# Cross attention of a decoder kernel: queries by three fp32r products instead of one fp32 product, with the tokens' rests on GpSimd

## The reference

```python
Q = (x @ Wq + bq)              # 4096 tokens x 256, 16 heads of 16
K, V = split(ctx @ Wkv + bkv)  # 4 x 77 tokens
attn = softmax(Q K^T * 16**-0.5 (+ mask))
x = layernorm(x + (attn V) @ Wo + bo)
```

## Time and profile before

| | |
|---|---|
| runs | 2994.00, 3000.15, 3001.02 us |
| median | 3000.15 us |
| the profiled execution's own time | 2996.25 us |
| its span in the profile | 2994.5 us |
| mean granted clock of PE | 0.942 of 2.4 GHz |

### The profile page before, as it was taken

How to read it: one execution, slowest core, us unless ns; L and a number is a source line. 1 busy time by engine, 2 the same in 40 slices (tenths; PEclk the granted TensorE clock), 3 DMA queues, 4 the chain that set the end, 5 groups by cost and what they waited for, 6 DMA issues and landing times. The chain is left out here.

```text
span 2994.5 us, 43256 instructions
## 1 busy us (share of the span) xinstructions
PE 2639.8 (88%) x11953; PEld 1603.3 (54%) x11953; DVE 1699.4 (57%) x3404; ACT 1175.7 (39%) x1644; POOL 1574.1 (53%) x1309
## 2 busy tenths in 40 slices
PE   7999999999999999999999968882796588788696
PEld 5666666666666666666666533432474244343254
DVE  5665665656666665665666634663234555468743
ACT  3443444444444444444444324541222334344234
POOL 3666766767766677676777731224333313222343
PEclk8999999999999999999999979996898599899798
DMA  6554455554556445455554320003894100000233
GB/s 174 115 130 111 105 121 114 120 116 110 113 114 135 108 111 120 106 121 114 122 115 106 68 82 9 2 2 116 334 339 144 45 0 1 30 2 9 49 124 91
DMA packets 407008, 303.17 MB, mean 101 GB/s; under 512 B 293559, under 2 KB 338911, under 8 KB 401791
## 3 DMA queue, kind: packets, MB, share of 16 engines
q1 hardware_dynamic: 390734, 231.17, 32.9%
q0 software_dynamic: 12224, 64.71, 6.1%
q10 hardware_dynamic: 3952, 6.08, 0.6%
HBM read 187.04 MB, written 94.39 MB: 94 GB/s over the span
## 5 line engine op out<-in xcount | busy, mean ns | idle before, releaser
L655 POOL TENSOR_TENSOR a_total<-a_total,a_pr 128x1024 f32<-128x1024 f32 x384 | 914.0, 2380 | 55.9 <-ACT a_pr L639 35.1
L639 ACT ACTIVATE a_pr<-a_psS 128x1024 f32<-128x1024 f32 x512 | 525.3, 1027 | 670.3 <-PE a_psS L627 666.5
L584 DVE TENSOR_REDUCE a_nmax<-a_psX 128x1 f32<-128x512 f32 x1024 | 695.4, 688 | 157.4 <-PE a_psX L579 155.8
L667 PE MATMUL a_psO<-a_pr,a_vd 128*64 128x512 f32 x2048 | 481.8, 602 | 0.0
L579 PE MATMUL a_psX<-a_kA,a_qA 128*128 128x512 f32 x1024 | 413.1, 405 | 25.6 <-issue 12.6
L655 POOL TENSOR_TENSOR a_total<-a_pr 128x1024 f32<-128x1024 f32 x64 | 153.5, 2399 | 482.0 <-ACT a_pr L639 482.0
L627 PE MATMUL a_psS<-a_qA,a_kA 128*128 128x512 f32 x1024 | 338.9, 412 | 2.7 <-DVE a_nT L600 1.4
L627 PE MATMUL a_psS<-a_qB,a_kB 128*128 128x512 f32 x1024 | 321.2, 395 | 0.0
L667 PEld LDWEIGHTS a_psO<-a_pr,a_vd 128*64 128x64 f32 x2048 | 129.9, 136 | 236.5 <-issue 179.3
L579 PEld LDWEIGHTS a_psX<-a_kA,a_qA 128*128 128x128 f32 x1024 | 194.0, 190 | 105.8 <-issue 35.9
L627 PEld LDWEIGHTS a_psS<-a_qA,a_kA 128*128 128x128 f32 x1024 | 180.9, 189 | 123.1 <-issue 90.1
(11 more groups left out here) (390 smaller groups left out, 4344.7 us busy)
## 6 DMA issues: line engine op xcount, KB each, us to landing
a_qA<-a_qhi SPq DMA_DIRECT2D x124, 256.0 KB
a_vd<-a_vg SPq DMA_DIRECT2D x128, 128.0 KB
a_kA<-a_khi SPq DMA_DIRECT2D x62, 256.0 KB
a_kA<-a_klo SPq DMA_DIRECT2D x62, 256.0 KB
a_kB<-a_khi SPq DMA_DIRECT2D x62, 256.0 KB
a_qB<-a_qlo SPq DMA_DIRECT2D x62, 256.0 KB
a_qhi<-a_ph SPq DMA_DIRECT2D x120, 128.0 KB, 3.1
a_qlo<-a_pl SPq DMA_DIRECT2D x120, 128.0 KB, 2.9
```

The lines of the kernel that those rows point to most:

```text
L584: w.eng.tensor_reduce(nmax[:, half, u:u + 1], psX[:, half, :], AX.X, ALU.max, negate=True)\
L639: w.eng.activation(pr[:, n, :], psS[:, half, :, :].rearrange("p a b -> p (a b)"), ACT.Exp, scale=SCALE)\
L655: w.eng.tensor_tensor(total[:, buf, :], first, pr[:, n, :], ALU.add).then_inc(sems["ad"], 1)
L667: last = w.eng.matmul(psO[q * HD:(q + 1) * HD, :], vd[:, b, kc, :], pr[:, n, q * 512:(q + 1) * 512], start=kc == 0, stop=kc == KC - 1)
```

## The change

In both cross attentions:

- `queries` no longer multiplies fp32 data. The weights and the turned tokens are each split into a part rounded to fp32r and the rest, and three products are summed in the bank: rounded weights by rounded tokens, rest of the weights by rounded tokens, rounded weights by the tokens' rest. That makes six matmuls of one pass where there were two of two passes.
- The weights are split once, in a new step `split_weights` after `turn_context`: ACT copies `wq` (128 x 1024) to `wqh`, POOL subtracts into `wql`.
- In `turn_x` ACT now copies the bank twice (to `xT` and, rounded, to `xh`), and POOL subtracts the two into `xl` for each half. `queries` waits on PE for `xl` of the second half (a semaphore of POOL), where it waited for ACT's copies.
- The four small POOL operations of `outputs` become a step of their own, `root`. For the first half it is called after `turn(1)` and thus stands on POOL behind the rests of both halves; for the second half it stays behind `put(1)`.
- To make room, `cx` lies in `xT`, and `wq` and `wk` in `oT`.

```diff
@@ -906,7 +906,7 @@
 
     with ExitStack() as ctx:
         m = Room(nc, ctx, tag)
-        wq, wk = (m.sb(n, [P, 2, NQ * P]) for n in ("wq", "wk"))
+        wqh, wql = (m.sb(n, [P, 2, NQ * P], F32R) for n in ("wqh", "wql"))
         wv, wo = (m.sb(n, [P, 2, D]) for n in ("wv", "wo"))
         bq, bk = (m.sb(n, [P, NQ]) for n in ("bq", "bk"))
         bqs, bks = (m.sb(n, [P, NQ]) for n in ("bqs", "bks"))
@@ -914,7 +914,6 @@
         bo = m.sb("bo", [P, D])
         ident = m.sb("ident", [P, P])
         sel0, sel17 = (m.sb(n, [P, 1]) for n in ("sel0", "sel17"))
-        cx = m.sb("cx", [TK, B, D])
         cxT = m.sb("cxT", [P, 2, B * TK])
         mraw = m.sb("mraw", [P, B * TK // 4], mybir.dt.int32)
         mbias = m.sb("mbias", [P, B, TK])
@@ -923,6 +922,10 @@
         kblk = m.sb("kblk", [P, NQ, B, NQ, TK], F32R)
         vP = m.sb("vP", [TK, B, H, R])
         xT = m.sb("xT", [P, 2, BT])
+        xh, xl = (m.sb(n, [P, 2, BT], F32R) for n in ("xh", "xl"))
+        cx = xT[0:TK, :, :].rearrange("p a b -> p (a b)").rearrange("p (b c) -> p b c", c=D)
         qF = m.sb("qF", [P, 3, NQ, BT])
         qR = m.sb("qR", [P, 2, NQ, BT], F32R)
         nmx = m.sb("nmx", [P, 4, H])
@@ -932,6 +935,7 @@
         inv = m.sb("inv", [P, BT // R])
         oC = m.sb("oC", [P, BT])
         oT = m.sb("oT", [P, 2, 2, BT])
+        wq, wk = oT[:, 0, :, :], oT[:, 1, :, :]
         xb = m.sb("xb", [P, 2, 2, D])
         res = m.sb("res", [P, 2, 2, D])
         bst = m.sb("bst", [P, 2, 2, 6])
@@ -944,7 +948,7 @@
         psS = m.ps("psS", [P, NQ, 512])
         psO = m.ps("psO", [P, 512])
         psM = m.ps("psM", [P, RB, 512])
-        names = ("cst", "cstv", "x", "cx", "wk", "wq", "wv", "wo", "mi", "m0", "m1", "m2", "k", "kf", "kb", "qr", "qm", "s",
+        names = ("cst", "cstv", "x", "cx", "wk", "wq", "wv", "wo", "wh", "wl", "xh", "xl", "mi", "m0", "m1", "m2", "k", "kf", "kb", "qr", "qm", "s",
                  "ex", "pv", "tk", "dv", "ot", "xb", "var", "pl", "rstd", "y")
         sems = {n: m.sem(n) for n in names}
         block = ctx.enter_context(nc.Block())
@@ -982,6 +986,15 @@
                 w.eng.tensor_copy(mb[:, :], psM[0:TK, k, 0:B * P:P]).then_inc(sems[f"m{k}"], 1)
             w.inc(f"m{k}")
             came["mask"] = (f"m{k}", w.at(f"m{k}"))
+        def split_weights(w):
+            if w.on("scalar"):
+                w.wait("wq", 16)
+                w.eng.activation(wqh[:, :, :], wq, ACT.Copy).then_inc(sems["wh"], 1)
+            if w.on("gpsimd"):
+                w.wait("wh", 1)
+                w.eng.tensor_tensor(wql[:, :, :], wq, wqh[:, :, :].bitcast(F32), ALU.subtract).then_inc(sems["wl"], 1)
 
         def keys(w):
             if w.on("tensor"):
@@ -1048,22 +1061,30 @@
                                                X[:, 4 * n + 2 * half + tt, cc * P:(cc + 1) * P], ident[:, :])
                 last.then_inc(sems["mi"], 1)
             w.inc("mi")
+            cols = slice(half * 256, (half + 1) * 256)
             if w.on("scalar"):
                 w.wait("mi", w.at("mi"))
-                w.eng.activation(xT[:, :, half * 256:(half + 1) * 256], psM[:, k, :].rearrange("p (a b) -> p a b", a=2), ACT.Copy)\
-                    .then_inc(sems[f"m{k}"], 1)
+                w.wait("xl", w.at("xl", 1))
+                w.eng.activation(xT[:, :, cols], psM[:, k, :].rearrange("p (a b) -> p a b", a=2), ACT.Copy).then_inc(sems["xh"], 1)
+                w.eng.activation(xh[:, :, cols], psM[:, k, :].rearrange("p (a b) -> p a b", a=2), ACT.Copy).then_inc(sems[f"m{k}"], 1)
+            w.inc("xh")
             w.inc(f"m{k}")
-            came["x", half] = (f"m{k}", w.at(f"m{k}"))
+            if w.on("gpsimd"):
+                w.wait("xh", w.at("xh"))
+                w.wait(f"m{k}", w.at(f"m{k}"))
+                w.eng.tensor_tensor(xl[:, :, cols], xT[:, :, cols], xh[:, :, cols].bitcast(F32), ALU.subtract).then_inc(sems["xl"], 1)
+            w.inc("xl")
 
         def queries(w, n, c):
             k = bank(w)
             if w.on("tensor"):
-                w.wait("wq", 16)
-                for half in range(2):
-                    w.wait(*came["x", half])
+                w.wait("wl", 1)
+                w.wait("xl", w.at("xl"))
                 w.wait(f"m{k}", w.at(f"m{k}"))
-                for cc in range(2):
-                    last = w.eng.matmul(psM[:, k, :], wq[:, cc, c * P:(c + 1) * P], xT[:, cc, :], start=cc == 0, stop=cc == 1)
+                for i, (wp, xp) in enumerate(((wqh, xh), (wql, xh), (wqh, xl))):
+                    for cc in range(2):
+                        last = w.eng.matmul(psM[:, k, :], wp[:, cc, c * P:(c + 1) * P], xp[:, cc, :],
+                                            start=i == 0 and cc == 0, stop=i == 2 and cc == 1)
                 last.then_inc(sems["mi"], 1)
             w.inc("mi")
             if w.on("scalar"):
@@ -1208,10 +1229,12 @@
                 w.inc("dv")
             w.inc(f"m{k}")
             w.inc("var")
+        def root(w, n, half):
             if w.on("gpsimd"):
                 if n or half:
                     w.wait("y", w.at("y"))
-                w.wait("var", w.at("var"))
+                w.wait("var", 2 * n + half + 1)
                 w.link(w.eng.tensor_tensor(rstd[:, half, 0, :], mv[:, half, :, 1], eps[:, :], ALU.add), "pl")
                 w.link(w.eng.tensor_tensor(rstd[:, half, 1, :], rstd[:, half, 0, :], mhalf[:, :], ALU.pow), "pl")
                 w.link(w.eng.tensor_tensor(rstd[:, half, 2, :], mv[:, half, :, 0], rstd[:, half, 1, :], ALU.mult), "pl")
@@ -1295,6 +1318,10 @@
                 if n:
                     outputs(w, n - 1, half)
 
+            def roots(half):
+                if n:
+                    root(w, n - 1, half)
             def norm(half):
                 if n:
                     normed(w, n - 1, half)
@@ -1311,6 +1338,7 @@
             scores(w, n, 1)
             big((0, 3))
             turn(1)
+            roots(0)
             big((1, 0), (1, 1))
             also(0)
             values(w, n, 0)
@@ -1325,6 +1353,7 @@
             values(w, n, 1)
             big((2, 3), (3, 0))
             put(1)
+            roots(1)
             big((3, 1), (3, 2))
             scores(w, n, 3)
             big((3, 3))
@@ -1344,6 +1373,7 @@
         def walk(w):
             for cc in range(2):
                 turn_context(w, cc)
+            split_weights(w)
             keys(w)
             for half in range(2):
                 turn_x(w, 0, half)
@@ -1372,6 +1402,7 @@
                 hall.load(w, 0)
             for half in range(2):
                 outputs(w, NB - 1, half)
+                root(w, NB - 1, half)
             for half in range(2):
                 normed(w, NB - 1, half)
             if hall is not None:
@@ -1380,8 +1411,8 @@
 
         @block.sync
         def _(eng):
-            eng.dma_start(cx[:, :, :], kv.rearrange("b k c -> k b c")).then_inc(sems["cx"], 16)
-            eng.dma_start(wk[:, :, :], w_k.rearrange("(a p) o -> p a o", p=P)).then_inc(sems["wk"], 16)
+            eng.dma_start(cx, kv.rearrange("b k c -> k b c")).then_inc(sems["cx"], 16)
+            eng.dma_start(wk, w_k.rearrange("(a p) o -> p a o", p=P)).then_inc(sems["wk"], 16)
             if y is not None:
                 eng.dma_start(X[:, 0:4, :], y.rearrange("(t p) c -> p t c", p=P)[:, 0:4, :]).then_inc(sems["x"], 16)
             eng.dma_start(wv[:, :, :], w_v.rearrange("(a p) o -> p a o", p=P)).then_inc(sems["wv"], 16)
@@ -1432,7 +1463,7 @@
                 eng.dma_start(t[:, :], src).then_inc(sems["wk"], 16)
             if mask is not None:
                 eng.dma_start(mraw[:, :], mask.partition_broadcast(P)).then_inc(sems["wk"], 16)
-            eng.dma_start(wq[:, :, :], w_q.rearrange("(a p) o -> p a o", p=P)).then_inc(sems["wq"], 16)
+            eng.dma_start(wq, w_q.rearrange("(a p) o -> p a o", p=P)).then_inc(sems["wq"], 16)
             eng.dma_start(wo[:, :, :], w_o.rearrange("(a p) o -> p a o", p=P)).then_inc(sems["wo"], 16)
             eng.dma_start(bo[:, :], b_o.partition_broadcast(P)).then_inc(sems["wo"], 16)
             eng.preload_act_table(ACT.Exp)
```

## The result

The changed kernel takes 3029.12 us (median of 4 runs, 3022.24 to 3033.45) where the kernel before takes 2997.07 us in the same session: a ratio of 1.0109, 95% interval [1.0095, 1.0124], 32 us more. The profiled execution took 3022.24 us, the fastest of its four.

A forecast was written before the change was run, and what follows sets the result against it. PE was taken to bound the stage, busy 24.8 of a block's 27.75 us. The chain's +14 us and the clock's +15 us gave +29 us: 3025 us profiled, 3029 us at the median, range 3003 to 3050 us.

The forecast's parts named there:

- Steps A to D: Blocks 1 to 5 of each attention: shorter queries save 1.36 us, waits for `xl` and `qF` lose 2.7: +1.3 a block.
- rival 3: POOL's subtraction is as quick as its rounding (0.61 us) and the clock holds: +7 us, 3007 us; chance 0.13.
- The start: Ahead of each attention's blocks: queries begin 2.4 us later for copies and subtractions, four calls give back 1.36: +1.0 us.
- Block 0 and block 6: In each attention: block 0, without `normed`, +0.3 us; block 6, inheriting only the shorter last queries, -0.7 us.
- The clock: PE's idling lets its clock fall to 0.50 at half of 14 places: 7 x 2.2 = +15 us.
- steps B and C: In a block: first `queries` wait for `xl`, 1.0 us later; the late root frees `qF`'s bank 1.65 us late.
- Rival 1: PE's clock stays up in both attentions: +14 us, 3014 us; chance 0.25.
- Rival 4: Rests ready before PE asks in each block: 21.8 us saved whole, less 2 for the start, 2980 us; chance 0.10.

The follow-up runs named there:

- root back: Changed kernel with the root called right behind `outputs` again, on POOL ahead of both rests: 3034.96 us, ratio 1.0132 to the kernel before.
- late wait: Changed kernel with PE waiting for `xl` only before the third product of `queries`: 3026.54 us, ratio 1.0109 to the kernel before.
- early turn: Changed kernel with the second half's transposes ahead of the second `scores`: 3008.65 us, ratio 1.0045 to the kernel before.
- the run with PE kept at work: Changed kernel, root left late, with six unread matmuls on PE before the wait for `xl`: 3018.05 us, ratio 1.0081 to the kernel before.
- the best order: Changed kernel with root back, late wait, both halves turned ahead of the second `scores`, scalings behind the queries' copy: 2980.09 us, ratio 0.9969.

## Why the prediction came out right, and where it did not

**Steps A to D.** Right, nearly to the tenth. Predicted: 2.0 us of idling for `xl`, measured 2.05; about 1.6 us for `qF`, measured 1.50; a block at full clock of 29.05, measured 29.11. POOL's subtraction took 1.26 to 1.28 us in the blocks, as the row with two operands said, which ended rival 3. The separate edits confirm the links: root back, the second wait goes; late wait, it moves; early turn, the first goes.

**The start.** The term of +1.0 us a start was mis-sized: it measured +4.0 and +3.4. I had PE's start 2.4 us late; in the first attention it was 2.9 late (1779.26 is 19.66 us behind the identity's first operation, at 1759.60; 1780.80 was 16.76 behind its own at 1764.04), since two subtractions beside DVE took 2.95 us, not 2.56; in the second it was 2.6 late. And the four calls gave nothing back: behind 3.89 us of idling the clock was at half for the first 3 us, as the window below shows, and the 24 passes took from 1779.26 to 1786.65, 7.4 us against 7.11 before. In the kernel without these rests they took 5.84 us at full clock, so 1.5 us of each start belong to the clock. The last 0.8 and 0.6 us I did not foresee: behind these queries PE waits for banks that ACT now copies twice, 0.89 and 0.67 us in the first attention (at 1789.32 and 1792.22) where it had waited 0.40 and 0.18 (at 1790.09 and 1792.50).

```profile
1779.20:1782.40 3.20, 3.14 (x8) 2.53 (x9) 3.01 (x7) 0.41 (x1) 0.00 (x0) 0.55 0.37 126
```

**Block 0 and block 6.** Predicted +0.3 and -0.7; the two block 0 were -1.6 and +0.4, and block 6 with what follows -1.1 and -1.9. Small, and they hide part of the start's error.

**The clock.** The number of falls was about right (7 of 14 places forecast, 9 found: both starts, blocks 2, 3 and 5 of the first attention and 1, 2, 4 and 5 of the second), the price was not. By the table, blocks 1 to 5 grew by 20.5 us in both attentions; ten times 1.36 is 13.6 of it, so the clock took some 7 us of these blocks, and with 3.1 in the starts some 10 us of the profiled execution, not 15. Two things were mis-sized. A short stretch at 0.50 (some 3 us) cost 0.2 to 0.4 us, in the blocks of 29.30 and 29.48; a long one (some 7 us) cost 1.8, in that of 30.94. I had 2.2 for all. The short ones were cheap because a wait took them up: in the block of 29.30 the slower queries came ahead of the wait for `qF`, which fell from 1.50 to 0.36 us (at 1908.84). And I priced block 1 as a new place, though it had the end of such a stretch in it already. The medians are 6 us further apart than the profiled executions (32 and 26 us); the changed kernel's runs spread over 11 us, and which of its blocks fall may differ between them, which no profile here shows.

**The sum.** Measured in the attentions: 13.6 for the ten blocks, 7.4 for the starts (3.1 of it the clock's), 7 for the clock in the blocks, -4.1 for blocks 0, 6 and the ends: 23.9, and 2.1 elsewhere. Forecast: +29, of which 14 by the chain and 15 by the clock. That the total came out near is luck, since errors stood against each other: the starts without their clock were forecast 2 us too small, the clock 5 too large, blocks 0 and 6 with the ends 3 too large, and 2 us elsewhere were not foreseen. The difference of the medians, 32 us, is not 29 either; 3029 us was hit to a tenth because the kernel before stood at 2997.07 beside it and not at 3000.15. The direction does not rest on luck but on steps B and C, which were sound.

**The rivals.** Rival 1 (the clock stays up, +14 us) is not what the run with PE kept at work gave: 3018.05 us look near its 3014, but the kernel before of that session took 2993.17, so it is +25. Of that the starts are 7.1 us, not 2, and 4 lie in three blocks of the second attention in which the clock was down even so. Rival 4 named the right condition, but not its worth: with the rests ready before PE asks, the ratio was 1.0045, with the root back and the late wait besides 0.998, and in the best order 0.9969. Its 20 us (0.7%) were not reached, since waits for banks came with the early turn. The row that spoke against it, ACT's exponential ahead of the second turn, was decisive: with the turn ahead of the scores, the wait for the rests late and the root back, blocks fell from 29.11 to 26.95 us.

## What to carry to other kernels

Before an operand is split to shorten PE's passes, trace how late its last part comes: here PE had 1.2 us a block less to do and idled 2.6 us more, and another order of the same work, with the wait for the rests put where they are read, turned a ratio of 1.0109 into 0.9969. Where a wait is taken away, look at what is queued behind it on ACT (here scalings behind a late root) and change both, since one alone only moves the idle time. And read a block's time beside its granted clock: if a shorter chain gives no shorter run, fill the idle time with unread matmuls once, to see the chain's own length.

## What the hardware showed that was not expected

- The same idling leaves the clock up in one block and not in another. In the changed kernel idle times of 2.05 and 1.50 us in the block from 1919.80 left it at 1.00; with the root back, 2.06 and 0.36 us took it to 0.50, in blocks of 30.84 us, in three blocks running. Less idling, more falls: the length of an idle time alone does not tell.
- In the blocks that ask, a stretch at 0.50 lasted some 3 or some 7 us (others some 10), and its length does not give its price. Stretches of some 3 us cost 0.2 to 0.4 us in the changed kernel, where a wait behind them shrank, and 1.6 us with the late wait, where they lay behind the last wait for ACT; PE was busy in nearly all of either (3.17 of 3.20 us from 1963.80, 3.00 of 3.00 from 1914.00 with the late wait). Stretches of some 7 us cost 1.8 and 2.6 us.
- POOL's subtraction into `xl` took a product of DVE from 0.42 us to 1.12, at 1933.77. The Trainium skill (page SBUF — State Buffer, "Who interferes with whom") says that a DVE instruction with two inputs in SBUF contends with a GpSimd instruction that reads SBUF; the trace agrees, with 559, 668 and 768 ns for the same DVE instruction with two inputs beside more and more work of POOL.
